# A graph-attention kernel: a block's small products, the end-node scan and the normalising placed one slot later in the planned order

## What is computed

```python
q = (x @ Wq + bq).reshape(n_nodes, 8, 16)        # k and v likewise
scores = sum(q[targets] * k[sources], -1) * 0.25 + (edge_features @ We + be)
max_s = segment_max(scores, targets)
e = exp(scores - max_s[targets])
denom = segment_sum(e, targets) + 1e-10
weighted = (e / denom[targets])[:, :, None] * v[sources]
agg = segment_sum(weighted, targets)
out = layernorm(x + agg @ Wo + bo)
```

## Time and profile before

| what | value |
|---|---|
| time, median of 3 runs (lowest, highest) | 2024.04 us (2020.06, 2025.88) |
| span of the profiled execution | 2449.4 us |
| busy: PE, PE weight load | 1545.6 us (63%), 1051.5 us (43%) |
| busy: DVE, ACT, POOL | 1370.8 us (56%), 454.6 us (19%), 1496.0 us (61%) |
| gathers: POOL L523 | 1536, 954 ns each |
| mean granted TensorE clock | 0.786 of full speed |

### The profile page before, as it was taken

The page is one execution under the profiler, slowest core; times in us unless marked ns, Lnnn a source line. Parts: engine busy times, 40 slices in busy tenths (PEclk is TensorE's granted clock), DMA queues, the critical chain, the costliest instruction groups (busy, mean ns, idle before and its releaser), DMA issues.

```text
span 2449.4 us, 25231 instructions
## 1 busy us (share of the span) xinstructions
PE 1545.6 (63%) x6655; PEld 1051.5 (43%) x6655; DVE 1370.8 (56%) x3214; ACT 454.6 (19%) x1496; POOL 1496.0 (61%) x1572
## 2 busy tenths in 40 slices
PE   5354576657665757566656666566766666666566
PEld 4233454435343434444444444344444444444344
DVE  4254575656555655555655656555555555556556
ACT  1011121212121211111111212111211212111112
POOL 4736546666666666666666666666666666666661
PEclk7677788868778777877887887877878778788878
DMA  6423334343334334343434343434334343434331
GB/s 248 160 84 105 94 101 130 107 123 115 118 117 130 109 108 130 107 131 108 129 108 128 111 129 108 128 108 125 112 113 127 110 128 111 126 111 127 108 106 31
DMA packets 115143, 288.11 MB, mean 118 GB/s; under 512 B 45909, under 2 KB 53856, under 8 KB 107960
## 3 DMA queue, kind: packets, MB, share of 16 engines
q0 software_dynamic: 74624, 203.26, 28.3%
q1 hardware_dynamic: 37628, 76.52, 9.4%
q10 hardware_dynamic: 2748, 6.69, 0.7%
HBM read 274.69 MB, written 11.67 MB: 117 GB/s over the span
## 4 chain that ended last, share of the span: by engine, by line
PE 40%; issue 25%; another core or an unknown queue 14%; DVE 10%; POOL 9%; DMA 1%; ACT 1%; DVEq 0%; ACTq 0%; POOLq 0%
PE ps_q L1230 14%; PE ps_a L1266 11%; POOL kv_buf L523 9%; PE ps_e L1242 2%; PE ps_t L1216 2%; PE ps_t L1210 2%; DVE prod L850 1%; DVE score L860 1%; DMA kv_buf<-kv_table,src_i 1%; PE ps_s L1294 1%; DVE wv L870 1%; PE ps_a L1319 1%; DVE run_fwd L912 1%; PE ps_a L1320 1%
## 5 line engine op out<-in xcount | busy, mean ns | idle before, releaser
L523 POOL DMA_INDIRECT kv_buf<-kv_table,src_i x1536 | 1465.6, 954 | 899.6 <-issue 407.5
L1230 PE MATMUL ps_q<-q_blk,hots 128*128 128x256 f32 x1564 | 566.4, 497 | 553.8 <-issue 553.6
L1230 PEld LDWEIGHTS ps_q<-q_blk,hots 128*128 128x128 f32 x1564 | 351.9, 246 | 677.7 <-issue 625.2
L1266 PE MATMUL ps_a<-wv,hots 128*128 128x272 f32 x1564 | 559.9, 490 | 8.5 <-issue 5.6
L613 ACT ACTIVATE hots<-ps_t 128x512 f32<-128x512 f32 x377 | 225.1, 597 | 1784.8 <-remote 1035.1
L850 DVE TENSOR_TENSOR prod<-ps_q,kv_buf 128x512 f32<-128x512 f32 (+1 forms) x392 | 268.7, 685 | 497.8 <-remote 322.7
L870 DVE TENSOR_TENSOR wv<-kv_buf,ps_w 128x512 f32<-128x512 f32 (+1 forms) x392 | 266.3, 679 | 238.8 <-remote 179.5
L1266 PEld LDWEIGHTS ps_a<-wv,hots 128*128 128x128 f32 x1564 | 335.4, 238 | 61.0 <-issue 10.4
L860 DVE TENSOR_REDUCE score<-prod 128x32 f32<-128x512 f32 (+1 forms) x392 | 267.2, 682 | 7.9 <-issue 0.2
L930 DVE TENSOR_TENSOR_SCAN ps_s<-seq_far,seq_left,ps_s 8x512 f32<-8x512 f32 x57 | 72.7, 1275 | 188.0 <-remote 155.0
L1309 PE MATMUL ps_a<-sums_sb,carry_from 128*1 128x136 f32 x112 | 28.0, 342 | 195.2 <-DVE sums_sb L982 154.8
(11 more groups left out here) (157 smaller groups left out, 1398.1 us busy)
## 6 DMA issues: line engine op xcount, KB each, us to landing
edge_f<-in_edge_blk SPq DMA_DIRECT2D x55, 1024.0 KB
kv_buf<-kv_table,src_i POOLq DMA_INDIRECT x1536
kv_table<-kv_buf ACTq DMA_DIRECT2D x12, 512.0 KB, 3.2
xt_blk<-in_x_t SPq DMA_DIRECT2D x114, 32.0 KB
out<-y_out SPq DMA_DIRECT2D x114, 32.0 KB
kv_buf<-in_x_perm SPq DMA_DIRECT2D x5, 512.0 KB
codes<-code_table SPq DMA_DIRECT2D x108, 10.5 KB
code_table<-kv_buf SPq DMA_DIRECT2D x1, 1344.0 KB
```

The source lines that it names most:

```text
L523: pool.indirect_dma_start(kv_buf[:, b % NBUF, t, :], None, kv_table, bass.IndirectOffsetOnAxis(ap=src_i[:, column:column + 1], axis=0)).th ...
L1230: one = pe.matmul(ps_q[q % 2][:, k * 2 * D:(k + 1) * 2 * D], hots[:, (v - 1) % 2, 0, k * P:(k + 1) * P], q_blk[:, b % QBUF, :], start=True ...
L1266: one = pe.matmul(sums(b), hots[:, (v - 1) % 2, 1, k * P:(k + 1) * P], wv[:, q % 2, 2 * k:2 * k + 2, :].rearrange("p j w -> p (j w)"), sta ...
```

## The change

No instruction is added, removed or resized; steps are placed elsewhere. Slots are those of the list above.

- `leave_over` moves from the head of PE's slot 1, ahead of `spread_q`, to its end, behind `turn_ends`; `scale_carry` moves from DVE's slot 1 to slot 2.
- `crossing_maxima` (DVE) moves from slot 1 to slot 2. `turn_ends` stays in slot 1, `turn_crossing` at the head of PE's slot 3, `edge_maxima` in slot 3.
- `turn_aggregate`, `copy_turned`, `finish_rows`, `copy_projected`, `moments_of_rows`, `inverse_deviation` and `normalise` all come one slot later.
- SLOTS has one more slot at its end, for the last `normalise`.

```diff
--- before.py
+++ after.py
@@ -369,7 +369,7 @@
 
             return FIRST[b] + sum(1 for t0, _ in STEP[b] if t0 < upto)
 
-        SLOTS = range(SLOT * (NB + 2) + LAG + 9)
+        SLOTS = range(SLOT * (NB + 2) + LAG + 10)
 
         def hots_in(v):
 
@@ -686,16 +686,16 @@
                         exponentials(chain(v, 4))
                     if chain(v, 6) is not None and chain(v, 6) + QBUF < NB:
                         copy_q(chain(v, 6) + QBUF)
-                    if at_node(v, 4) is not None:
-                        copy_turned(at_node(v, 4))
                     if at_node(v, 5) is not None:
-                        copy_projected(at_node(v, 5))
+                        copy_turned(at_node(v, 5))
+                    if at_node(v, 6) is not None:
+                        copy_projected(at_node(v, 6))
                     if step_in(v - SLOT - LAG) is not None:
                         copy_weights(step_in(v - SLOT - LAG))
                     if chain(v, -4) is not None:
                         copy_terms(chain(v, -4))
-                    if at_node(v, 7) is not None:
-                        inverse_deviation(at_node(v, 7))
+                    if at_node(v, 8) is not None:
+                        inverse_deviation(at_node(v, 8))
             with act.Else():
                 turn = act.alloc_register("turn_act")
                 act.reg_mov(turn, 0)
@@ -1017,12 +1017,12 @@
                         weigh(step_in(v - SLOT - LAG))
                     if step_in(v) is not None:
                         multiply(step_in(v))
-                    if at_node(v, 3) is not None and at_node(v, 3) + 1 < NB:
-                        scale_carry(at_node(v, 3) + 1)
+                    if at_node(v, 4) is not None and at_node(v, 4) + 1 < NB:
+                        scale_carry(at_node(v, 4) + 1)
                     if chain(v, 0) is not None:
                         run_maxima(chain(v, 0))
-                    if chain(v, 1) is not None:
-                        crossing_maxima(chain(v, 1))
+                    if chain(v, 2) is not None:
+                        crossing_maxima(chain(v, 2))
                     if chain(v, 3) is not None:
                         edge_maxima(chain(v, 3))
                     if step_in(v) is not None:
@@ -1032,10 +1032,10 @@
                     if at_node(v, 2) is not None:
                         add_folded(at_node(v, 2))
                         divide(at_node(v, 2))
-                    if at_node(v, 6) is not None:
-                        moments_of_rows(at_node(v, 6))
-                    if at_node(v, 8) is not None:
-                        normalise(at_node(v, 8))
+                    if at_node(v, 7) is not None:
+                        moments_of_rows(at_node(v, 7))
+                    if at_node(v, 9) is not None:
+                        normalise(at_node(v, 9))
             with dve.Else():
                 for i in (1, 2):
                     for g in range(GS[i]):
@@ -1326,8 +1326,6 @@
                     project_q(b)
                 match(-1)
                 for v in SLOTS:
-                    if at_node(v, 3) is not None and at_node(v, 3) + 1 < NB:
-                        leave_over(at_node(v, 3) + 1)
                     if chain(v, 3) is not None:
                         turn_crossing(chain(v, 3))
                     if step_in(v) is not None:
@@ -1349,10 +1347,12 @@
                         project_q(chain(v, 5) + QBUF)
                     if at_node(v, 2) is not None:
                         fold_halves(at_node(v, 2))
-                    if at_node(v, 3) is not None:
-                        turn_aggregate(at_node(v, 3))
+                    if at_node(v, 3) is not None and at_node(v, 3) + 1 < NB:
+                        leave_over(at_node(v, 3) + 1)
                     if at_node(v, 4) is not None:
-                        finish_rows(at_node(v, 4))
+                        turn_aggregate(at_node(v, 4))
+                    if at_node(v, 5) is not None:
+                        finish_rows(at_node(v, 5))
             with pe.Else():
                 turn = pe.alloc_register("turn_pe")
                 pe.reg_mov(turn, 0)
```

## The result

The changed kernel takes 2029.41 us in the median of its runs (2027.36 to 2032.5), the kernel before, beside it, 2023.64 (2019.06 to 2026.43). The ratio is 1.0036, with a 95% interval of 1.0027 to 1.0044: some 7 us slower, where no change was forecast. The time lies inside the range, 5.4 us above the point.

What follows compares the result with a forecast made beforehand. POOL's issuing was taken as the bound: 63.8 us start + 1920.0 gathers + 43.6 tail = 2027.4, near the median 2024.04. All terms of the change were 0, giving 2024 us, range 2009 to 2040.

Steps and rivals of the forecast that it cites:

- POOL's issuing is the bound of the main blocks: Main blocks: in a plain run POOL issues gathers almost without stop, 1536 at 1.25 us, 1920.0 us.
- the 23.2 that I had allowed: Setup: without DVE's idle time there, a plain run's gathers could start up to 23.2 us earlier.
- Rival one: A plain run holds POOL waiting caused by the old order; 2004 to 2018, middle 2012 us; chance 0.18.
- Left-over row worth nothing: PE slot 1: removing the wait for add_folded gains 0, as POOL's pace covered it with 2.7 us to spare.
- The scan, 0: Scan moved to slot 2: slot 3's spreading still ends 2.1 or 1.1 us early, so the new wait costs 0.
- Rival two: `drop` comes late and delays slot 5's gather in every held block; slower, 2050 us; chance 0.12.
- DVE, 0: DVE's moved instructions cost 0, covered by 11 us of free time in a block.
- Rows, SP, 0: Rows, Wo and normalising one slot later, and SP's loads and stores 5 us later, cost 0.
- Tail, -1 to +2, taken 0: After the last gather, paced by PE, DVE and ACT: change bounded by -1 and +2 us, taken as 0.
- Rival three: PE sets the pace of a plain run too; time falls to 1829 to 1986 us; chance 0.02.
- What would show it: Signs in the changed profile: gathers 1.25 us apart, L1309 wait under 15, `drop` wait 30 to 150, span 2380 to 2460.

Runs made afterwards that it cites:

- e_scan_only: Kernel before with only the scan over end nodes one slot later, in all blocks: 2022.11 us, ratio 1.0000.
- e_early_new_tail: Kernel before with the changed placement in the last three blocks alone, old placement in blocks 0 to 53: 2021.32 us, ratio 0.9994.
- e_rows_only_2: Kernel before with only the rows (turn, carried row, Wo, moments, normalising) one slot later in all blocks, repeated on another chip: 2022.70 us, ratio 1.0000.
- e_rows_left_2: Kernel before with left-over row, carried row and rows later in all blocks, scan at its old place, repeated on another chip: 2024.45 us, ratio 1.0007.
- e_late_old_tail: Changed kernel with the old placement put back in the last three blocks: 2027.17 us, ratio 1.0022 to the kernel before.
- e_late_fill_2: Changed kernel plus 8 unread filling matmuls a block ahead of PE's waits, sixth to last block, repeated on another chip: 2025.82 us, ratio 1.0019 to before.

## Why the prediction was wrong, step by step

Two terms that the prediction took at 0 were mis-sized. The tail, bounded by -1 and +2 us, lengthened by about 4 to 5 with POOL's last waits, and the clock of PE there was in no term. DVE's instructions, which were only asked whether they find room, lengthened POOL's gathers by about 2 us.

- **POOL's issuing is the bound of the main blocks: right.** Gathers start 1.25 us apart and POOL does not wait. In the sum the terms were off and cancelled. The first gather starts at 42.72, not 63.8, 21.1 us earlier, nearly all of the 23.2 that I had allowed; the 1536 gathers take 1937.0 us (1979.70 - 42.72), not 1920.0, for 10.7 us of them are lengthened ones and 6.3 POOL's waits in the last stretch; and from the last gather to the end it is 47.8, not 43.6. I had read the agreement of 2027.4 with the median as proof that POOL never waits. It was partly luck.
- **Rival one (a plain run hides POOL's waiting): wrong.** The setup is as short as its bound, and no waiting stands in the main blocks of before.
- **Left-over row worth nothing: right for its own slot.** The wait at L1309 fell from 321.6 to 6.4 us, and rows and left-over row together cost at most 0.16%, the upper end of the interval. Beside the moved scan it is not free: putting it back in the changed kernel took the ratio from 1.0035 to 1.0015.
- **The scan, 0: right by itself** (1.0000). PE's new wait for `drop` is 132.4 us, inside the 30 to 150 forecast. The spreading of slot 3 is at half clock in 43 of the 47 blocks 6 to 52 and ends 1.94 us (median) ahead of its gather, 1.2 to spare after the 0.75 of hand-over, where 1.1 was forecast. I had not looked at slot 4, the tighter one in some blocks: 1.12 us, 0.4 to spare. Rival two did not come, but by less than I thought.
- **DVE, 0: wrong by some 2 us.** I asked only whether DVE's instructions find room, and not what they do to POOL while they run. edge_maxima lies beside a gather in every order; what the change moved is the instant. Its L957 begins 0.05 to 0.25 us ahead of a gather's start in 38 blocks instead of 10 (last section), and at those places 43 gathers are long instead of 20, 5.2 us instead of 2.5. POOL is the bound, so each tenth of a microsecond counts in full.
- **Rows, SP, 0: right** (1.0000 for the rows alone).
- **Tail, -1 to +2, taken 0: this term was mis-sized.** The last stretch is 64.0 to 66.5 us in the three profiles at the full loss; in those at the level of before it is 58.5 to 61.2, but for the one exception. Counted from the last gather's end, as the prediction does, it is 47.6 to 50.2 us, against 43.9 to 45.7 in e_scan_only, e_early_new_tail and e_rows_only_2 (e_rows_left_2 has 47.4). The rest is POOL's waits for PE before that, 6.3 to 6.6 us against 3.4 to 6.2, which the sum had at nothing. I had counted instructions and their order there, and had named PE, DVE and ACT as what paces the stretch; PE's clock was in no term. A wait of PE that costs nothing while POOL sets the pace can cost twice where PE does: once itself, and once in the half clock behind it. The second part goes with the loss in the profiles and is not shown by a time.
- **Together** some 2 us of gathers and, from 59 or 60 us, 4 to 5 of last stretch make 6 to 7, about the loss measured. The two sizes come from single profiles. No single part has it: the scan alone, the rows alone and the last three blocks alone cost nothing, and in their profiles PE is busy for 7.41, 7.92 and 6.49 of the 8 us ahead.
- **Rival three (PE the bound): wrong** over the main blocks: 157 us more of PE's busy time there moved POOL's way to the cut by 1.9. The Trainium skill (Perfetto Trace Analysis, section Optimization Strategy) says that a kernel may have regimes in which the most contended engine changes; here the rows show POOL first and PE in the last 64 us (PE busy 45.8 of them, DVE 38.6), and I had asked for the bound only once.
- **What would show it.** Right: gathers 1.25 apart, the wait at L1309 under 15 us, the new wait, the scan behind the product (1958.70 behind 1957.82). Wrong: a span of 2380 to 2460; that was the level of the first profile (last section). And the plain time moved by 5.8 us by the medians and by 7 by the ratio, on both sides of the 6 us that I had set for "wrong".

What stays open: how much of the last stretch's loss the half clock makes and how much the waits themselves, since the run made for it fell on a pausing chip; and where exactly the 5 us of e_late_old_tail and the 3 us of e_late_fill_2 lie. Their profiles are of executions 2.4 and 2.9 us quicker than the median, the second the quickest of its twelve, so a short last stretch in them does not tell.

## What to carry to other kernels

Ask for the bound of each stretch, and above all of the last one: a wait that is free under another engine's pace is dear where the waiting engine sets it, and here half clock for PE's matmuls came behind it. Where POOL's gathers are the bound, look at what DVE runs beside them, and at which instant, and not only at whether POOL waits. Before a profile is compared with another, see how far its own execution lies from the median of its kernel. When a profile's span is a fifth above the plain runs, take none of its setup or tail terms into a sum that is to tell 0.3%.
